# The last stage of a four-layer kernel on one core: experts by sorted blocks of tokens in place of all experts for all tokens

## The reference

```
scores = softmax(h @ gate_w.T)                # 8 experts
idx    = top_k(scores + gate_bias, 2)         # two experts for each token
y      = sum over the two: scores[e] * (silu(h @ w1[e].T) * (h @ w3[e].T)) @ w2[e].T      # inner width 128
z      = (silu(h @ sw1.T) * (h @ sw3.T)) @ sw2.T                                          # shared, inner width 256
out    = x + y + z
```

## Time and profile before

| | us |
|---|---|
| median of 3 runs | 1230.58 (1227.54 to 1233.87) |
| the profiled execution's own time | 1230.32 |
| its span, first to last instruction | 1228.2 |
| TensorE busy in the span | 1017.8 (83%) |
| VectorE / ScalarE / GpSimd busy | 900.3 / 643.2 / 354.2 |
| mean granted TensorE clock | 0.922 of full speed (2.4 GHz; the lower level is 1.2 GHz, shown as 0.50) |

### The profile page before, as it was taken

One profiled execution on the slowest core, in us unless ns is written; L12 is line 12 of the kernel. 1 busy time (PEld: TensorE's weight loads), 2 busy tenths in 40 slices (PEclk: granted clock), 3 DMA queues, 4 the chain that ended last, 5 costly groups with the idle time before them and its releaser, 6 DMA issues.

```text
span 1228.2 us, 21187 instructions
## 1 busy us (share of the span) xinstructions
PE 1017.8 (83%) x7331; PEld 655.1 (53%) x7331; DVE 900.3 (73%) x2273; ACT 643.2 (52%) x1031; POOL 354.2 (29%) x334
## 2 busy tenths in 40 slices
PE   5868800589979997899679999998889889999998
PEld 3653300554546774454226777775645456666665
DVE  4586699847885763778588898898578876666666
ACT  3424578846643455564277777775466533333332
POOL 5610000101210004444298999993112200000000
PEclk9899955779999998999769999998899999999999
DMA  7000000010000000000000000000000000000000
GB/s 274 1 1 1 1 0 0 1 66 1 2 2 1 1 1 1 1 2 2 1 1 1 1 0 0 0 0 1 1 1 2 2 2 9 9 9 9 9 9 18
DMA packets 8958, 13.50 MB, mean 11 GB/s; under 512 B 816, under 2 KB 6704, under 8 KB 8624
## 3 DMA queue, kind: packets, MB, share of 16 engines
q1 hardware_dynamic: 8880, 12.46, 3.0%
HBM read 10.36 MB, written 2.10 MB: 10 GB/s over the span
## 4 chain that ended last, share of the span: by engine, by line
PE 44%; DVE 24%; issue 7%; ACT 4%; DVEq 0%; ACTq 0%
DVE big L785 7%; DVE hq L780 7%; PE psum L558 5%; PE psum L2203 5%; PE psum L2200 5%; PE psum L2217 5%; PE psum L1520 2%; DVE big L2042 2%; PE psum L1763 2%; PE psum L1771 2%; PE psum L512 2%; PE psum L1774 2%; PE psum L1537 2%; PE psum L1778 2%; DVE big L789 2%
## 5 line engine op out<-in xcount | busy, mean ns | idle before, releaser
L780 DVE TENSOR_REDUCE hq<-psum 128x16 f32<-128x1024 f32 x96 | 114.4, 1220 | 80.1 <-PE psum L512 43.1
L1952 POOL TENSOR_TENSOR big<-big 128x512 f32<-128x512 f32 x128 | 128.6, 1045 | 21.1 <-ACT big L1857 21.1
L2250 ACT ACTIVATE big<-psum 128x512 f32<-128x512 f32 x80 | 47.8, 598 | 141.1 <-PE psum L2200 140.9
L422 POOL TENSOR_TENSOR big<-big,w_const 128x256 f32<-128x256 f32 x48 | 36.6, 763 | 264.9 <-PE psum L558 228.8
L1880 ACT ACTIVATE psum<-big,tmp 128x512 f32<-128x512 f32 x128 | 84.9, 686 | 25.0 <-DVE big L2042 22.4
L2042 DVE SCALAR_TENSOR_TENSOR big<-big,tmp,psum 128x512 f32<-128x512 f32 x128 | 90.4, 743 | 4.8 <-ACT psum L1880 1.9
L2271 DVE TENSOR_TENSOR big<-big,psum 128x512 f32<-128x512 f32 x80 | 54.4, 687 | 52.1 <-PE psum L2203 50.4
L668 ACT ACTIVATE big<-psum 128x1024 f32<-128x1024 f32 x64 | 62.0, 1021 | 53.3 <-PE psum L542 53.3
L785 DVE RECIPROCAL big<-psum 128x256 f32<-128x256 f32 x48 | 84.0, 1749 | 7.4 <-PE psum L558 7.3
L2217 PEld LDWEIGHTS psum<-tmp,big 128*128 128x128 f32 x512 | 66.6, 192 | 40.3 <-issue 38.0
L2203 PE MATMUL psum<-hT,tmp 128*128 128x512 f32 x160 | 82.7, 599 | 2.6 <-DVEq L2261 2.6
(11 more groups left out here) (243 smaller groups left out, 2353.8 us busy)
## 6 DMA issues: line engine op xcount, KB each, us to landing
out<-X SPq DMA_DIRECT2D x8, 256.0 KB, 2.3
tmp<-in_pack_f SPq DMA_DIRECT2D x1, 1924.0 KB, 7.4
w_f<-in_pack_f SPq DMA_DIRECT2D x1, 1280.0 KB, 12.3
tmp<-in_pack_once SPq DMA_DIRECT2D x1, 960.0 KB, 6.9
X<-in_x SPq DMA_DIRECT2D x1, 768.0 KB, 5.3
w_a<-in_pack_a SPq DMA_DIRECT2D x3, 256.0 KB, 7.7
w_a<-in_pack_a SPq DMA_DIRECT2D x1, 704.0 KB, 9.7
w_f<-in_pack_f SPq DMA_DIRECT2D x1, 576.0 KB, 4.9
```

The lines of the kernel that those rows point to most:

```text
L780: dve.tensor_reduce(nm, psum[:, 1 + 2 * t:3 + 2 * t, :].rearrange("p c (r l k) -> p (c r) l k", r=2, k=SK), AX.X, ALU.max, negate=True).th ...
L1952: ins = pool.tensor_tensor(ssum[t][:, h * 512:(h + 1) * 512].rearrange("p (i j) -> p i j", i=ROWS2), st[:, 0, h, 0:ROWS2].unsqueeze(2).to_ ...
```

## The change

The two shared halves are still computed for all tokens by groups of 512. The eight gated experts no longer are. Instead the tokens are sorted by their pair of chosen experts (28 unordered pairs). Each pair's tokens fill whole blocks of 128 rows in a DRAM table `rows3`; for every possible filling 59 blocks are enough, and the program always runs 59, whatever the gates say. A row of 260 words (1040 bytes) holds the normalised token, the token plus the shared experts' output, its two gates and its number. All of the table is first filled with zero rows whose number lies outside of the output.

Step by step:

- All groups are normalised (two on ACT beside the one that the early part has, three on POOL, one on DVE and the early one), turned and given logits before any expert runs. The gates of tiles 0 to 23 and of 24 to 31 are then one chain each on DVE, with `max_index` beside `max`, the pair's number, and a one-hot matrix M3 of 28 columns per tile.
- Counts per pair and tile (32 products of one column), prefix sums on DVE, first block of every pair, and each token's place (`places`) follow, with DVE and PE taking turns. Two products give the table tab3: for every block the offsets of its two experts' weights. The shared work of groups 0 to 2 is written in between these steps, that of groups 3 to 7 behind them.
- POOL writes the rows to their places with 32 indirect transfers of 128 rows, each group's after its `add`. SP waits for all of them, then loads the blocks one by one (133 KB each, up to 4 in flight, 8 slots).
- In a block PE turns 128 tokens, loads two register values from tab3, does w1 and w3 of each of the two experts in one 256-column product whose weight address is a register, turns the two hidden tiles, and does two products with w2. ACT copies the turned tokens, takes the silu of 128x256 and copies the turned hidden tiles. DVE makes the hidden tiles with the gate as a scalar (two instructions) and adds the row's stored sum. POOL sends each block to the output with an indirect transfer by the tokens' numbers, at most 4 in flight; filler rows are skipped by the bounds check.
- The block loop is written out, 59 times, as a pipeline over four iterations: turn of block i, up of i-1, turning of hidden of i-2, down of i-3.
- POOL also does one memset and one iota in stage a0, SP fills the table after the weights' loads, and three semaphores of f0 become one (`f0_next`).

The core of the diff:

```diff
@@ PACKS @@
-    "f3": [("f3_gate", E3), ("f3_w1", CH3 * P), ("f3_w3", CH3 * P), ("f3_w2", CH3 * P)],
+    "f3": [("f3_gate", E3), ("f3_w", E3 * 3 * P), ("f3_s1", 2 * P), ("f3_s3", 2 * P),
+           ("f3_s2", 2 * P), ("f3_tri", P), ("f3_exp", E3), ("f3_pair", PAIRS3), ("f3_blk", 60), ("f3_lohi", 2),
+           ("f3_tri28", PAIRS3)],
@@ att0_pool @@
+            pool.memset(pad3[:, :], 0.0).then_inc(S("f3_pad"), 1)
+            pool.wait_ge(S("f3_pad"), 1)
+            pool.iota(pad3[:, ID3:ID3 + 1].bitcast(U32), [[0, 1]], base=1 << 20, channel_multiplier=0)\
+                .then_inc(S("f3_pad"), 1)
@@ f3 @@
+        def f3_pool(pool):
...
+            for g in ON_POOL:
+                f3_ln_ready(pool, g)
+                for t in range(4 * g, 4 * g + 4):
+                    ins = pool.tensor_scalar(rowbuf[:, t, 0:P], X[:, t, :], mean[:, t:t + 1], rstd[:, t:t + 1],
+                                             ALU.subtract, ALU.mult)
+                ins.then_inc(S("f3_nP"), 1)
+
+            pool.wait_ge(S("f3_m"), 6)
...
+            for t in range(N_TILES):
+                if t % GT == 0:
+                    pool.wait_ge(S("f3_x"), t // GT + 1)
+                pool.indirect_dma_start(dram["rows3"], bass.IndirectOffsetOnAxis(place3[:, t:t + 1], 0),
+                                        rowbuf[:, t, :], None).then_inc(S("f3_sent"), 16)
+
+            for j in range(NB3):
+                pool.wait_ge(S("f3_x"), N_GROUPS + j + 1)
+                if j >= 4:
+                    pool.wait_ge(S("b_so%d" % (j % 4)), 16 * (j // 4))
+                pool.indirect_dma_start(dram["out"], bass.IndirectOffsetOnAxis(slot3[j % RS][:, ID3:ID3 + 1].bitcast(U32), 0),
+                                        out3[j % RS], None, bounds_check=B * SQ - 1, oob_is_err=False)\
+                    .then_inc(S("b_so%d" % (j % 4)), 16)
...
+        def f3_sp(sp):
+            sp.wait_ge(S("f3_sent"), 16 * N_TILES)
+            for j in range(NB3):
...
+                sp.dma_start(slot3[j % RS], dram["rows3"][j * P:(j + 1) * P, :]).then_inc(S("b_in%d" % (j % 4)), 16)
 
         def f3_pe(pe):
...
+            f3_turn(pe, 1)
+            for g in range(2, N_GROUPS):
+                f3_turn(pe, g)
+                f3_logits(pe, g - 1)
+            f3_logits(pe, N_GROUPS - 1)
+            pe.wait_ge(S("f3_hT"), N_GROUPS)
+            up(0, 0)
+            up(0, 1)
+            up(1, 0)
+            down(0)
+            up(1, 1)
+            counts()
+            up(2, 0)
+            down(1)
+            firsts()
+            up(2, 1)
+            places()
+            for g in range(3, N_GROUPS):
+                up(g, 0)
+                up(g, 1)
+                down(g - 1)
+            down(N_GROUPS - 1)
...
+            for i in range(NB3 + 3):
+                if i < NB3:
+                    j = i
+                    pe.wait_ge(S("b_in%d" % (j % 4)), 16 * (j // 4 + 1))
+                    if j >= 2:
+                        pe.wait_ge(S("f3_hT"), N_GROUPS + j - 1)
+                    pe.transpose(bank(j % 2)[:, 0:P], slot3[j % RS][:, 0:P], ident).then_inc(S("f3_tn"), 1)
+                if 1 <= i <= NB3:
+                    j = i - 1
+                    first[j] = [nc.values_load(tab3[0:1, 64 * k + j:64 * k + j + 1], engines=[mybir.EngineType.PE],
...
+                                for k in range(2)]
+                    pe.wait_ge(S("f3_hT"), N_GROUPS + j + 1)
+                    if j >= 2:
+                        pe.wait_ge(S("f3_hid"), 2 * N_GROUPS + 2 * j - 2)
+                    for k, r in enumerate(first[j]):
+                        ins = pe.matmul(bank(2 + j % 2)[:, 2 * P * k:2 * P * (k + 1)], hTb[j % 3],
+                                        W["f3_w"][:, ds(r, 2 * P)], start=True, stop=True)
+                    ins.then_inc(S("b_u"), 1)
+                if 2 <= i <= NB3 + 1:
+                    j = i - 2
+                    pe.wait_ge(S("f3_hid"), 2 * N_GROUPS + 2 * j + 2)
+                    if j >= 2:
+                        pe.wait_ge(S("b_hidT"), j - 1)
+                    for k in range(2):
+                        ins = pe.transpose(bank(4 + 3 * (j % 2))[:, k * P:(k + 1) * P], hidb[j % 2][:, k * P:(k + 1) * P],
+                                           ident)
+                    ins.then_inc(S("b_th"), 1)
+                if i >= 3:
+                    j = i - 3
+                    pe.wait_ge(S("b_hidT"), j + 1)
+                    if j >= 2:
+                        pe.wait_ge(S("f3_x"), N_GROUPS + j - 1)
+                    for k, r in enumerate(first[j]):
+                        ins = pe.matmul(bank(5 + j % 2)[:, 0:P], hidTb[j % 2][:, k * P:(k + 1) * P],
+                                        W["f3_w"][:, ds(r + 2 * P, P)], start=(k == 0), stop=(k == 1))
+                    ins.then_inc(S("f3_y"), 1)
...
         def f3_dve(dve):
...
+            gates(0)
+            gates(1)
+            hid(0, 0)
+            hid(0, 1)
+            hid(1, 0)
+            add(0)
...
@@ sync @@
-            with sp.Fori(0, N_GROUPS) as g:
...
+            sp.wait_ge(S("f3_pad"), 2)
+            sp.dma_start(dram["rows3"].rearrange("(b p) n -> p b n", p=P),
+                         pad3[:, :].unsqueeze(1).to_broadcast([P, NB3, ROW3])).then_inc(S("ld_rows"), 16)
+            f3_sp(sp)
```

More of the change, by code:

```diff
@@ L2120, in f2_dve @@
                 a3.mx(b, 1)
-        f3 = Carve()
-        f3.at = f3.limit - 2304
-        p3 = [f3.take(GT * E3) for _ in range(2)]
-        w3b = f3.take(GT * E3)
-        top3 = f3.take(GT * 8).rearrange("p (t k) -> p t k", t=GT)
-        s3 = f3.take(GT * 4).rearrange("p (i t) -> p i t", i=4)
-        gate3 = f3.take(GT * E3)
-        sil3 = [f3.take(512) for _ in range(2)]
-        hid3 = [f3.take(512) for _ in range(2)]
-        def f3_bank(g):
-            return bank(5 if isinstance(g, int) and g == 0 else 7)
@@ L2139, in f3_logits @@
-        def f3_logits(pe, g, j):
-            pe.wait_ge(sem("f3", "hT"), at("f3", "hT") + g + 1)
-            if isinstance(g, int) and g == 0:
+        rowbuf = big[:, 2 * HALF - N_TILES * ROW3 - 512:2 * HALF - 512].rearrange("p (t n) -> p t n", n=ROW3)
+        f3 = Carve(2 * HALF - N_TILES * ROW3 - 512)
+        hT3 = [hT[:, 0, :], hT[:, 1, :]] + [f3.take(GN) for _ in range(N_GROUPS - 2)]
+        sil3 = [f3.take(GN) for _ in range(2)]
+        hid3 = [f3.take(GN) for _ in range(4)]
+        prob3 = f3.take(N_TILES * E3).rearrange("p (t e) -> p t e", e=E3)
@@ new lines, in build @@
+        M3 = f3.take(N_TILES * PAIRS3, BF16).rearrange("p (t k) -> p t k", k=PAIRS3)
+        pm3 = [f3.take(16 * PAIRS3).rearrange("p (t k) -> p t k", k=PAIRS3) for _ in range(2)]
+        D3 = f3.take(N_TILES * PAIRS3).rearrange("p (t k) -> p t k", k=PAIRS3)
+        pre3 = [f3.take(16 + N_TILES + 1) for _ in range(2)]
+        base3 = f3.take(N_TILES)
+        nb3, st3, en3, st128 = (f3.take(2) for _ in range(4))
+        nb3i = f3.take(2).bitcast(I32)
+        ge3, oh3 = f3.take(60), f3.take(60)
@@ new lines, in build @@
+        tri16 = f3.take(P, BF16)
+        ones16 = f3.take(2, BF16)
+        ones28 = f3.take(P)
+        tab3 = f3.take(128).bitcast(I32)
+        RS = 8
+        slots = Carve(6 * GN)
+        slot3 = [slots.take(ROW3) for _ in range(RS)]
+        hTb = [f3.take(P) for _ in range(3)]
+        silb = [f3.take(2 * P) for _ in range(2)]
+        hidb = [f3.take(2 * P) for _ in range(2)]
+        hidTb = [f3.take(2 * P) for _ in range(2)]
+        out3 = [f3.take(P) for _ in range(RS)]
+        PARTS3 = ((0, EARLY), (EARLY, N_TILES))
@@ new lines, in f3_norm_act, with f3_turn @@
+        def f3_norm_act(act, g):
+            f3_ln_ready(act, g)
+            for t in range(4 * g, 4 * g + 4):
+                ins = act.activation(rowbuf[:, t, 0:P], X[:, t, :], ACT.Identity, scale=rstd[:, t:t + 1],
+                                     bias=shifted[:, t:t + 1])
+            ins.then_inc(S("f3_nA"), 1)
+        def f3_turn(pe, g, free=None):
+            f3_normed(pe, g)
+            if free is not None:
+                pe.wait_ge(*free)
+            if g >= 2:
+                pe.wait_ge(S("f3_hT"), g - 1)
+            for t in range(GT):
+                ins = pe.transpose(bank(g % 2)[:, t * P:(t + 1) * P], rowbuf[:, 4 * g + t, 0:P], ident)
+            ins.then_inc(S("f3_tn"), 1)
@@ L2142, in f3_logits, with f3_take @@
+        def f3_take(act, g):
+            act.wait_ge(S("f3_tn"), g + 1)
+            act.activation(hT3[g], bank(g % 2), ACT.Copy).then_inc(S("f3_hT"), 1)
+        def f3_logits(pe, g):
+            pe.wait_ge(S("f3_hT"), g + 1)
+            if g == 0:
                 pe.wait_ge(S("ld_f3"), 16)
-            else:
-                pe.wait_ge(S("f3_p"), g)
+            if 4 * g == EARLY:
+                pe.wait_ge(sem("a3", "res"), at("a3", "res") + N_GROUPS + 1)
+            part = int(4 * g >= EARLY)
```

434 lines of the change are left out of this document (280 added, 154 removed).

## The result

The changed kernel took 1220.08 us (median of 10 runs) against 1228.15 us before (10 runs): ratio 0.9915, 95% interval 0.9897 to 0.9934. That is faster by 0.85%, where the forecast of 1205 us meant 2.1%; the time lies inside the range of 1184 to 1268 us. One run of the ten, 1673.69 us at a granted clock of 0.55, was disturbed and is in no comparison.

The account below looks back on a forecast made before the run. TensorE streaming fp32 columns was taken as the bound. Blocks start at 1074.3, plus 121.0 for 59 blocks, 3 for pipeline fill, 4.5 for the end: span 1202.8, plus 2.1 gives 1205 us; range 1184 to 1268.

Parts of the forecast that it names:

- rival 3: Scatter and blocks: GpSimd becomes the bound at 2.36 us an indirect transfer instead of 1.1, giving 1262 us; chance 0.15.
- One norm, a turn and the logits of the last part put the gates' start at 998: End of a3: last layer norm step at 995.2, then this work on the last part, so gates start at 998 us.
- 3 us for a clock that falls because TensorE idles in the gates: Shared rest: 3 us added for a lowered clock after TensorE's idling, taking its end from 1061.9 to 1065.
- 4.5 for the last add, transfer and end: Kernel's end: 4.5 us from the last add, read from the kernel before plus GpSimd's 1.1 us.
- only the last four stand out: Scatter: at 1.1 us each, four transfers fit a group's 5.2 us; only four follow the shared work, ending at 1069.4.
- the sign of a wrong scatter step: Scatter: the step is wrong if its last transfer is issued later than 5 us after the last shared add.
- Gates and counts: From the gates' start at 998 through counts and places to the scatter's start at 1032.5: 34.5 us.
- TensorE's idle time in the gates: Between the third up and the next: the gates step is wrong if this is far from 14 us.
- The pitch, 2.05: Block loop: 2.05 us a block, from 1.65 for array or sequencer plus one handover; 121.0 us for 59 blocks.
- a whole handover of 0.41: Block loop: one of four handovers between engines charged in full, 0.41 us a block.
- Rival 2: Block loop: register loads of 0.6 us in PE's sequencer make a block 2.45 to 2.65, 1228 to 1240 us; chance 0.17.
- rival 4: Block loop: dear register loads of 1.28 us make a block 3.6 to 4.0, 1294 to 1318 us; chance 0.12.

Follow-up runs that it names:

- combo_end_again: combo_end, same program, run once more beside the changed kernel and the kernel before on one chip: 1205.73 us, ratio to before 0.9808.
- take_first: The changed kernel with ACT's copies of turned groups 1 and 2 moved ahead of the layer norm's finish: 1216.82 us, ratio to before 0.9891.
- up_early: The changed kernel with the first shared up product moved directly behind the turn of group 1 on TensorE: 1213.8 us, ratio to before 0.9874.
- static_addr: The changed kernel without register loads, every block using experts 0 and 1 from fixed addresses: 1206.45 us, one run.
- four_loads: The changed kernel with both table entries loaded a second time ahead of each block's down, four register loads a block: 1247.48 us, one run.
- combo_end: The changed kernel with take_first's and up_early's moves, places ahead of most shared work, and last output waits on SP: 1212.01 us, ratio to before 0.9858.

## Why the prediction was off

1. **The direction and the main mechanism held.** The gated experts' time went, the blocks came at about the array's pace, and no rival came true in full; of rival 3 only its direction did, in the scatter, where GpSimd's pace is 1.27 us a transfer in place of 2.36. The measured time is 15 us above the forecast: in the table four steps were too small and two too large, so the sum also had some luck.
2. **"One norm, a turn and the logits of the last part put the gates' start at 998" failed, by 7.8 us.** The path was wrong. The first gates need tiles 0 to 23, not the last part; they stand behind the turns of groups 1 to 6 and the logits of groups 1 to 5 on TensorE, which `f3_pe` puts out behind a3's last product. At full clock and without a wait these take some 7.7 us (combo_end_again: 9.4 less 1.7 for `up(0, 0)`), which would give about 998.5 here: that the wrong path gave nearly this number was luck. What the number lacked is 2.5 us of wait for ACT, whose copy stood behind the layer norm's finish (take_first took it away), and nearly 5 us for groups at 2.46 us at half clock, where rows 3 promised 1.2. I had charged 3 us for a clock that falls because TensorE idles in the gates. It fell before them: in the changed kernel just behind the 2.5 us wait, in take_first and up_early without a wait of that length.
3. **The end, "4.5 for the last add, transfer and end", was short by 7.5 us.** It was read from the kernel before, which ends with SP's transfers; the change lets GpSimd end the kernel, and its DRAIN costs 0.082 us for each of 91 transfers. Nothing in the trace of before has this price, but that the last engine would be another one was in the change, and the step named no cost for it. (Its own terms, 3.7 and 1.1, add up to 4.8.)
4. **The scatter, "only the last four stand out", failed by 3.9 us.** The duration was taken as 1.1 us and measured 0.97, but a gap of 0.30 us comes with each, so the pace was 1.27. And eight transfers stood out, not four, because the last two adds come 1.8 us apart: 8 x 1.27 less 1.8 is about the 8.3 us measured behind the last add's end, in place of 4.4. The last transfer was issued 7.4 us behind that end, beyond the 5 us that the prediction named as the sign of a wrong scatter step.
5. **Gates and counts** (34.5 against 37.2) were right within 8%, at a lower clock (0.67 to 0.71 from 1010 to 1030) than in rows 3. TensorE's idle time in the gates was 5.9 us and not 14, another sign that the prediction named: it reached the shared products only at 1009.7 and did them at half clock. The gates themselves took 15.5 us to the first hidden tile, for 14.2 forecast, so the sign stands for the late start and not for their length.
6. **The pitch, 2.05, came out at 1.95**, one of the two steps that erred the other way (the other is landing and first load, 3.8 for 4.9). The two bounds that it weighed were good: the array alone gives 1.70 (static_addr) against 1.65, and a register load is 0.304 us against the 0.3 taken. The step added a whole handover of 0.41 between engines on top; what static_addr takes away is 0.24, and with it go the loads, so what was added to the array's pace is loads and not a handover.
7. Rival 2 rested on a load of 0.6 us, and the Trainium skill (DMA: Bandwidth & Descriptors, Latency and other measured facts) has about 600 ns as the floor of a tensor load. The trace disagrees: a one-value load from SBUF by TensorE's queue takes 0.30 us, and 0.54 to 1.00 come only with two to four values. At the page's figure the changed kernel would have been no faster than before, by an estimate from four_loads: it spends about that time in loads, four of 0.30 us a block, and took 1247.48 us. The times of rival 4, 1294 to 1318 us, are spans; its sum leaves out the 2.1 us between span and time.

**For other kernels.** When a change hands the end of a kernel to another engine, ask what that engine still does after its last instruction, and look at the closing instructions of its queue: here GpSimd paid for every transfer that it had issued in the program. Price a chain of equal instructions by the distance of their starts, not by their duration. And when narrow work that used to be scattered between wide products is gathered in one place, expect that the clock can fall there though TensorE looks busy.

## What the runs showed of the hardware

- GpSimd's closing DRAIN, once its work was done: 0.054 us without transfers, 0.134 with one, 6.77 with 82, 7.50 with 91, plain and indirect alike.
- A load of register values from SBUF in TensorE's queue: 0.30, 0.54 and 1.00 us for one, two and four values.
- An indirect transfer of 128 rows keeps GpSimd 0.96 to 0.98 us (the first of a kind 1.31) and the next starts 0.30 later; a plain one of 128 x 4 bytes 0.54.
- A stretch of 128-column transposes and 8-column products in which TensorE had no gap was granted 0.66 over ten microseconds and ended at the 1.2 GHz level (combo_end); another execution of the same program kept 1.00 some 6 us longer before it fell. The same stretch with a 512-column product behind each group's logits was granted 1.00 (2.4 GHz) throughout, in one execution.
- While 91 small transfers were landing, TensorE and DVE stood still for 2 to 10.7 us with nothing to wait for, and a 256 KB transfer took 24.7 us in place of 2.3; in the scatter of some groups of runs there were stops of 2 to 4 us. The cause of either was not tested.
